# Joining the two transposes of a block and their ScalarE copies in a gated attention kernel

## The chip, the cores and the metric

The kernel runs on one core of one Trainium2 chip. The metric is the device time of one execution in microseconds, given as the median of several runs. The engines are named as the profile names them: PE is TensorE's matmul, PEld its weight load, DVE is VectorE, ACT is ScalarE, POOL is GpSimd, SP issues the DMAs.

## What is computed

The input `x` has 16 batches of 64 channels by 512 positions; the context has the same shape. Everything is fp32. Cut to what matters:

```python
# attention, per batch: q = layernorm(x), k = c = s = context
qp = Wq @ instance_norm(q) + bq            # 64 x 512
kp = Wk @ instance_norm(k) + bk
sp = Ws @ s + bs_
attn = softmax(qp^T @ kp, axis=-1)         # 512 x 512
mean, mean_sq = attn-weighted sums of sp and of sp*sp
x = x + tanh(g_xattn) * (instance_norm(c) * sqrt(relu(mean_sq - mean**2)) + mean)
# feed-forward with a dequantised 512 x 512 weight
x = x + tanh(g_ffn) * (layernorm(x) @ w.T)
```

## The kernel before

Two batches of 64 channels fill the 128 partitions, so there are 8 tiles `t` (`TILES`), each with batches `b` = 0 and 1. The 512 query positions of a tile are cut into 4 blocks `j` of 128 (`JC`), which gives 32 pairs `g = 4t + j` (`PAIRS`); a pair is one block of queries for both batches. Each engine runs its own hand-written instruction list strictly in order, and semaphores order the engines against each other.

For one pair: `scores(g)` on PE (line 250) writes 128x1024 scores, both batches side by side, into one of two two-bank PSUM tiles; `maximum(g)` on DVE (line 558) reduces both halves in one instruction; `exponentials(g, b)` on ACT (line 394) writes `probs` and its row sum, one batch at a time; `reciprocal(g, b)` on DVE and `normalise_probs(g, b)` on POOL divide by the sum; `turn(g, b)` on PE (line 265) transposes the four 128x128 blocks of one batch into the bank `turn_bank[b]`; `keep_turned(g, b)` on ACT (line 403) copies that bank into `probs_t`; and one tile later `weigh(t, b, i)` on PE (line 275) multiplies `probs_t` with the values. Four `weigh` calls make the sums of one batch of a tile, which `keep_sums` (line 411) copies out.

The lists interleave the pairs. In the loop step `g`:

- PE runs, where `j` is even, `scores(g+2)` and `scores(g+3)`; then `project_q` (`j` = 0), `project_k` (`j` = 1) or `value_product` (`j` = 2); then `turn(g, 0)` and `turn(g, 1)`, and two `weigh` calls of the tile before. Where `j` is odd, one `weigh` stands between the two turns and one behind them.
- ACT runs `keep_sums` (`j` = 0 and 2), `keep_q_hi` (`j` = 0, it waits for `project_q`) or `keep_k_hi` (`j` = 1); then `exponentials(g+2, 0)`, `keep_turned(g, 0)`, `exponentials(g+2, 1)`, `keep_turned(g, 1)`.
- DVE runs `reciprocal(g+1, 1)`, then `maximum(g+2)`, then the statistics and splits of later tiles.

So `maximum` of a pair stands behind the reciprocal of batch 1 of the pair before, and that reciprocal waits for `exponentials(.., 1)` of that pair. `scores(g)` waits until `exponentials(g-2, 1)` has read its score tile (`exp_done`, line 256). `turn(g, b)` waits until the copy of the same bank, one pair earlier, is done (line 269). After the loop come the last sums, the roots, the second layer norm and the feed-forward (`turn_y`, `feed_forward`), whose `y` and `result` tiles lie in `probs_t`.

In the first pairs the lists are written out by hand (lines 303 to 314 on PE): `scores(2)`, `turn(0, 0)`, `scores(3)`, `turn(0, 1)`, `project_k_plain(1)`, `turn(1, 0)`, `turn(1, 1)`; on ACT `keep_k_hi(1)` stands between `keep_turned(1, 0)` and `exponentials(3, 1)` (line 447), and `scores(4)` waits for `keep_k_lo(1)` on DVE, which waits for that `keep_k_hi(1)`.

Of the kernel before, what the change touches and what calls it, by code (L numbers as in the profile page):

```python
# [14 lines left out]
P = 128  # L15


def gated_attention_ffn(nc, x, context, params, weight_q_t, scales_zeros, out):


    BATCHES, C, N = x.shape
    TILES = BATCHES // 2
    JC = N // P
    PAIRS = JC * TILES
# [3 lines left out]
    PROBS = 6  # L28
# [8 lines left out]
    with ExitStack() as ctx:  # L37
        def sb(name, shape, dt=F32):
            return ctx.enter_context(nc.sbuf_tensor(name, shape, dt))

        def banks(name, n=1):
            return ctx.enter_context(nc.psum_tensor(name, [P, n * 512], F32))

        def sem(name):
            return ctx.enter_context(nc.semaphore(name))
# [29 lines left out]
        probs = [sb(f"probs{i}", [P, N]) for i in range(PROBS)]  # L75
        neg_max = sb("neg_max", [P, 4, 2])
        den = sb("den", [P, 4, 2])
        rden = sb("rden", [P, 4, 2])
        probs_t = [[sb(f"probs_t{i}{b}", [P, JC, N]) for b in range(2)] for i in range(2)]
        values = [sb(f"values{i}", [P, JC, 2, 2, C]) for i in range(2)]  # L80
        mean_sq = sb("mean_sq", [P, N])

        ident = sb("ident", [P, P])
# [12 lines left out]
        rstd2 = sb("rstd2", [P, TILES])  # L96
        shift2 = sb("shift2", [P, TILES])

        y = [probs_t[0][0][:, i, :] for i in range(4)]
        result = [probs_t[0][1][:, i, :] for i in range(4)]  # L100
        yt_hi = q_hi
        yt_lo = q_lo

        score = [banks(f"score{i}", 2) for i in range(2)]
        turn_bank = [banks(f"turn_bank{i}") for i in range(2)]
        pv_bank = banks("pv_bank")
        proj_bank = banks("proj_bank")
        ffn_bank = [score[i][:, n:n + 512] for n in (0, 512) for i in range(2)]
# [41 lines left out]
        probs_done = sem("probs_done")  # L150
        turned = sem("turned")
        turned_kept = sem("turned_kept")
        pv_done = sem("pv_done")
# [30 lines left out]
        def sums_bank(t, b):  # L184
            return proj_bank if (t, b) == (TILES - 1, 0) else pv_bank
# [34 lines left out]
        def _(pe):  # L220
# [41 lines left out]
                                         k[n][half(b), :], start=(n == 0), stop=(n == 2))  # L262
                last.then_inc(scores_done, 1)

            def turn(g, b):
                c = 2 * g + b
                pe.wait_ge(probs_done, c + 1)
                if c >= 2:
                    pe.wait_ge(turned_kept, c - 1)
                for i in range(JC):  # L270
                    last = pe.transpose(turn_bank[b][:, P * i:P * i + P],  # L271
                                        probs[c % PROBS][:, P * i:P * i + P], ident[:, :])
                last.then_inc(turned, 1)

            def weigh(t, b, i):
                if i == 0:
                    pe.wait_ge(turned_kept, 2 * (JC * t + JC - 1) + b + 1)
                    pe.wait_ge(s_squared, t + 1)
                    if sums_bank(t, b) is proj_bank:
                        pe.wait_ge(s_kept, t + 1)  # L280
                    elif (t, b) == (0, 0):
                        pe.wait_ge(k_lo_done, 1)
                    else:
                        pe.wait_ge(sums_kept, min(2 * (2 * t + b), 4 * (TILES - 1)))
                mm = pe.matmul(sums_bank(t, b)[:, :], values[t % 2][:, i, b, :, :].rearrange("p a c -> p (a c)"),  # L285
                               probs_t[t % 2][b][:, i, :], start=(i == 0), stop=(i == JC - 1))
                if i == JC - 1:
                    mm.then_inc(pv_done, 1)

# [16 lines left out]
            scores(1)  # L306
            project_q_plain(1)
            scores(2)
            turn(0, 0)
            scores(3)  # L310
            turn(0, 1)
            project_k_plain(1)
            turn(1, 0)
            turn(1, 1)
            pe.wait_ge(w_split, 1)

            for t in range(TILES):
                for j in range(JC):
                    g = JC * t + j
                    if g < 2:  # L320
                        continue
                    if j % 2 == 0 and g + 2 < PAIRS:
                        scores(g + 2)
                        scores(g + 3)
                    if j == 0 and t + 1 < TILES:
                        project_q(t + 1)
                    if j == 1 and t + 1 < TILES:
                        project_k(t + 1)
                    if j == 2:
                        value_product(t)  # L330
                    turn(g, 0)
                    if t > 0 and j % 2 == 1:
                        weigh(t - 1, j // 2, 2)
                    turn(g, 1)
                    if t > 0 and j % 2 == 1:
                        weigh(t - 1, j // 2, 3)
                    if t > 0 and j % 2 == 0:
                        weigh(t - 1, j // 2, 0)
                        weigh(t - 1, j // 2, 1)

            def turn_y(u):
                pe.wait_ge(y_done, u + 1)
                if u < 2:
                    pe.wait_ge(turned_kept, 2 * PAIRS)
                else:
                    pe.wait_ge(yt_lo_done, u - 1)
                for g in range(GROUPS):
                    last = pe.transpose(turn_bank[u % 2][:, P * g:P * g + P], y[u % 4][:, P * g:P * g + P],
                                        ident[:, :])
                last.then_inc(y_turned, 1)  # L350
# [30 lines left out]
        def _(act):  # L381
# [18 lines left out]
                               bias=neg_max[:, g % 4, b:b + 1],  # L400
                               accum_out=den[:, g % 4, b:b + 1]).then_inc(exp_done, 1)

            def keep_turned(g, b):
                t, j = g // JC, g % JC
                act.wait_ge(turned, 2 * g + b + 1)
                if j == 0 and t >= 2:
                    act.wait_ge(pv_done, 2 * (t - 2) + b + 1)
                act.copy(probs_t[t % 2][b][:, :, P * j:P * j + P],  # L408
                         turn_bank[b][:, :].rearrange("p (i n) -> p i n", i=JC)).then_inc(turned_kept, 1)

            def keep_sums(t, b):
                act.wait_ge(pv_done, 2 * t + b + 1)
# [6 lines left out]
            def root(u):  # L419
                act.wait_ge(relu_done, u + 1)  # L420
                act.activation(VAR[:, u, :], VAR[:, u, :], ACT.Sqrt).then_inc(root_done, 1)  # L421
# [11 lines left out]
            for t in range(TILES):  # L433
                for j in range(JC):
                    g = JC * t + j
                    if j == 0 and t >= 2:
                        keep_sums(t - 2, 1)
                    if j == 2 and t >= 1:
                        keep_sums(t - 1, 0)
                    if j == 0 and 0 < t < TILES - 1:  # L440
                        keep_q_hi(t + 1)
                    if j == 1 and 0 < t < TILES - 1:
                        keep_k_hi(t + 1)
                    if g + 2 < PAIRS:
                        exponentials(g + 2, 0)
                    keep_turned(g, 0)
                    if g == 1:
                        keep_k_hi(1)
                    if g + 2 < PAIRS:
                        exponentials(g + 2, 1)  # L450
                    keep_turned(g, 1)
                    if g == PAIRS - 2:
                        root(0)

# [472 lines left out]
```

## Time and profile before

| | us |
|---|---|
| median of 3 runs | 179.69 |
| lowest and highest of them | 179.33, 180.91 |
| the profiled execution | 180.87 |
| its span, first to last instruction | 178.7 |

The span is what the trace shows; 2.17 us of the profiled execution lie around it. Starts in the trace are counted in us from the start of the span. Instructions on one engine overlap a little, so the distance between two starts, not the duration of one row, tells what an instruction costs its queue. The end of a matmul is modelled. A wait is put down to what came last.

### The profile page before, as it was taken

How to read it: one execution, taken by the hardware profiler on the slowest of the kernel's cores; microseconds unless marked ns; L12 is line 12 of the kernel's file. 1: busy time of each engine (PE TensorE's matmuls, PEld its weight loads, DVE VectorE, ACT ScalarE, POOL GpSimd, SP SyncE). 2: the span in 40 equal slices, each digit the busy share in tenths (PEclk: the TensorE clock that was granted, in tenths of full speed). 3: DMA queues.
4: the chain of work that ended last, by engine and by line, in shares of the span. 5: the costliest groups of instructions: out<-in, count | busy, mean ns of one | idle time of the engine just before them, and what ended most of it. 6: DMA issues, size and time to landing. Idle time of an engine off the chain costs nothing.

```text
span 178.7 us, 2695 instructions
## 1 busy us (share of the span) xinstructions
PE 164.8 (92%) x832; PEld 108.1 (60%) x832; DVE 136.8 (77%) x277; ACT 123.3 (69%) x268; POOL 131.4 (74%) x155
## 2 busy tenths in 40 slices
PE   6768596999999999999999999999999999998992
PEld 6335473756667566656666575667656546866881
DVE  2899757776699779977987997777567579999941
ACT  2439737787788888778778887796889987723410
POOL 1407729656969997998899799996889899994100
PEclk9999969999999999999999999999999999999999
DMA  5991013005000400310000000000000000101323
GB/s 167 354 397 72 0 44 133 4 2 176 0 0 4 178 0 0 109 71 0 2 4 2 0 0 0 0 4 0 0 0 2 0 0 4 54 5 71 129 97 117
DMA packets 4717, 9.83 MB, mean 55 GB/s; under 512 B 480, under 2 KB 608, under 8 KB 4704
## 3 DMA queue, kind: packets, MB, share of 16 engines
q1 hardware_dynamic: 4704, 9.67, 14.9%
q8 instruction: 7, 0.11, 0.3%
q14 instruction: 6, 0.05, 0.1%
HBM read 7.57 MB, written 2.10 MB: 54 GB/s over the span
## 4 chain that ended last, share of the span: by engine, by line
PE 69%; DVE 14%; POOL 8%; ACT 5%; issue 2%; DMA 1%; ACTq 0%; POOLq 0%
PE pv_bank L285 25%; PE score L261 13%; PE turn_bank L271 13%; PE proj_bank L295 5%; ACT probs L399 3%; DVE X L687 2%; PE score L362 2%; POOL CTX L858 2%; DVE neg_max L560 2%; DVE stats L692 2%; PE score L358 2%; PE score L359 2%; DVE probs_t L711 2%; DMA X<-in_x 1%; POOL rstd L862 1%
## 5 line engine op out<-in xcount | busy, mean ns | idle before, releaser
L768 POOL TENSOR_SCALAR probs<-probs,rden 128x512 f32<-128x512 f32 x64 | 51.8, 815 | 12.1 <-DVE rden L565 12.1
L285 PE MATMUL pv_bank<-probs_t,values 128*128 128x512 f32 x120 | 58.8, 594 | 0.4 <-ACT VAR L417 0.4
L399 ACT ACTIVATE probs<-score,neg_max 128x512 f32<-128x512 f32 x64 | 44.3, 692 | 18.7 <-DVE neg_max L560 18.7
L560 DVE TENSOR_REDUCE neg_max<-score 128x2 f32<-128x1024 f32 x32 | 38.6, 1209 | 3.9 <-PE score L261 3.9
L271 PEld LDWEIGHTS turn_bank<-ident,probs 128*128 128x128 f32 x256 | 30.7, 142 | 16.1 <-issue 13.6
L408 ACT COPY probs_t<-turn_bank 128x512 f32<-128x512 f32 x64 | 37.4, 586 | 2.5 <-PE turn_bank L271 2.5
L271 PE MATMUL turn_bank<-ident,probs 128*128 128x128 f32 x256 | 36.3, 275 | 0.9 <-ACT probs_t L408 0.9
L285 PEld LDWEIGHTS pv_bank<-probs_t,values 128*128 128x128 f32 x120 | 19.4, 191 | 8.8 <-issue 8.8
L261 PE MATMUL score<-k_hi,q_hi 64*128 64x512 f32 x64 | 14.7, 450 | 5.8 <-DVE k_lo L554 3.6
L565 DVE RECIPROCAL rden<-den 128x1 f32<-128x1 f32 x64 | 9.6, 151 | 10.5 <-ACT probs L399 10.2
L261 PEld LDWEIGHTS score<-k_hi,q_hi 64*128 64x128 f32 x64 | 6.1, 183 | 18.0 <-issue 10.8
L358 PE MATMUL score<-w_hi,q_hi 128*128 128x512 f32 x32 | 13.2, 414 | 0.2 <-ACT q_hi L468 0.2
L261 PE MATMUL score<-k_hi,q_lo 64*128 64x512 f32 x64 | 13.1, 400 | 0.0
L261 PE MATMUL score<-k_lo,q_hi 64*128 64x512 f32 x64 | 13.0, 396 | 0.0
L399 ACT ACTIVATION_READ_ACCUMULATOR probs<-score,neg_max 128x1 f32 x64 | 12.9, 202 | 0.0
L359 PE MATMUL score<-w_lo,q_hi 128*128 128x512 f32 x32 | 12.7, 396 | 0.0
L461 ACT ACTIVATE probs_t<-X,shift,rstd 128x512 f32<-128x512 f32 x8 | 6.5, 817 | 7.4 <-POOL shift L865 7.3
L745 POOL TENSOR_TENSOR rstd<-var_eps,power 128x1 f32<-128x1 f32 x8 | 4.4, 550 | 9.3 <-DVE var_eps L507 9.3
L858 POOL TENSOR_TENSOR CTX<-CTX,VAR 128x512 f32<-128x512 f32 x8 | 10.7, 1332 | 0.7 <-ACT VAR L421 0.6
L749 POOL TENSOR_TENSOR rstd<-var_eps,power 128x1 f32<-128x1 f32 x8 | 6.3, 788 | 6.1 <-DVE var_eps L516 6.1
L787 POOL TENSOR_TENSOR VAR<-VAR,mean_sq 128x512 f32<-128x512 f32 x8 | 10.6, 1323 | 0.2
L548 DVE SCALAR_TENSOR_TENSOR q_lo<-proj_bank,params_sb,q_hi 128x512 fp32r<-128x512 f32 x8 | 6.0, 750 | 6.1 <-ACT q_hi L386 6.1
(85 smaller groups left out, 298.3 us busy)
## 6 DMA issues: line engine op xcount, KB each, us to landing
X<-in_x SPq DMA_DIRECT2D x8, 256.0 KB, 5.3
raw_ctx<-in_context SPq DMA_DIRECT2D x8, 256.0 KB, 2.7
sz<-in_scales_zeros SPq DMA_DIRECT2D x4, 512.0 KB, 3.7
out<-probs_t SPq DMA_DIRECT2D x8, 256.0 KB, 2.0
w_int<-in_weight_q_t SPq DMA_DIRECT2D x1, 1024.0 KB, 8.3
params_sb<-in_params SPq DMA_DIRECT2D x1, 226.0 KB, 3.9
```

Source lines behind the costliest of these rows:

```text
L261: last = pe.matmul(score[g % 2][:, N * b:N * b + N], q[n][half(b), P * j:P * j + P], k[n][half(b), :], start=(n == 0), stop=(n == 2))
L271: last = pe.transpose(turn_bank[b][:, P * i:P * i + P], probs[c % PROBS][:, P * i:P * i + P], ident[:, :])
L285: mm = pe.matmul(sums_bank(t, b)[:, :], values[t % 2][:, i, b, :, :].rearrange("p a c -> p (a c)"), probs_t[t % 2][b][:, i, :], start=(i = ...
L358: pe.matmul(ffn_bank[u % 4], hi, w_hi[:, g, :], start=(g == 0), stop=False)
L359: pe.matmul(ffn_bank[u % 4], hi, w_lo[:, g, :], start=False, stop=False)
L399: act.activation(probs[c % PROBS][:, :], score[g % 2][:, N * b:N * b + N], ACT.Exp, bias=neg_max[:, g % 4, b:b + 1], accum_out=den[:, g % ...
L408: act.copy(probs_t[t % 2][b][:, :, P * j:P * j + P], turn_bank[b][:, :].rearrange("p (i n) -> p i n", i=JC)).then_inc(turned_kept, 1)
L560: dve.tensor_reduce(neg_max[:, g % 4, :], score[g % 2][:, :].rearrange("p (b m) -> p b m", b=2), AX_X, ALU.max, negate=True).then_inc(max_ ...
L565: dve.reciprocal(rden[:, g % 4, b:b + 1], den[:, g % 4, b:b + 1]).then_inc(rden_done, 1)
L768: pool.tensor_scalar(probs[c % PROBS][:, :], probs[c % PROBS][:, :], rden[:, g % 4, b:b + 1], 1.0, ALU.mult, ALU.mult).then_inc(probs_done, 1)
L787: pool.tensor_tensor(VAR[:, t, :], VAR[:, t, :], mean_sq[:, :], ALU.subtract).then_inc(var_done, 1)
L858: pool.tensor_tensor(CTX[:, u, :], CTX[:, u, :], VAR[:, u, :], ALU.mult).then_inc(scaled_done, 1)
```

## The change

The two turns of a pair become one function that waits once for `turned_kept` and then runs the eight transposes in a row, batch 0 into the first and batch 1 into the second of two neighbouring banks (`turn_banks`). `keep_turned(g)` is one ACT copy of both banks, 128x1024, in place of two of 128x512, and it waits until both batches are turned. The `probs_t` tiles of both batches become one tile. The copy stands where the first of the two copies stood, between the two exponentials. `turned_kept` now counts pairs. On PE, where `j` is odd, both `weigh` calls follow the turns; in the first pairs `turn(0, 1)` moves ahead of `scores(3)`.

```diff
-        probs_t = [[sb(f"probs_t{i}{b}", [P, JC, N]) for b in range(2)] for i in range(2)]
+        probs_t = [sb(f"probs_t{i}", [P, 2, JC, N]) for i in range(2)]
...
-        turn_bank = [banks(f"turn_bank{i}") for i in range(2)]
+        turn_banks = banks("turn_banks", 2)
+        turn_bank = [turn_banks[:, 512 * i:512 * i + 512] for i in range(2)]
...
-            def turn(g, b):
-                c = 2 * g + b
-                pe.wait_ge(probs_done, c + 1)
-                if c >= 2:
-                    pe.wait_ge(turned_kept, c - 1)
-                for i in range(JC):
-                    last = pe.transpose(turn_bank[b][:, P * i:P * i + P],
-                                        probs[c % PROBS][:, P * i:P * i + P], ident[:, :])
-                last.then_inc(turned, 1)
+            def turn(g):
+                if g >= 1:
+                    pe.wait_ge(turned_kept, g)
+                for b in range(2):
+                    c = 2 * g + b
+                    pe.wait_ge(probs_done, c + 1)
+                    for i in range(JC):
+                        last = pe.transpose(turn_bank[b][:, P * i:P * i + P],
+                                            probs[c % PROBS][:, P * i:P * i + P], ident[:, :])
+                    last.then_inc(turned, 1)
...
-                    pe.wait_ge(turned_kept, 2 * (JC * t + JC - 1) + b + 1)
+                    pe.wait_ge(turned_kept, JC * t + JC)
...
             scores(2)
-            turn(0, 0)
+            turn(0)
             scores(3)
-            turn(0, 1)
             project_k_plain(1)
-            turn(1, 0)
-            turn(1, 1)
+            turn(1)
...
-                    turn(g, 0)
-                    if t > 0 and j % 2 == 1:
-                        weigh(t - 1, j // 2, 2)
-                    turn(g, 1)
-                    if t > 0 and j % 2 == 1:
-                        weigh(t - 1, j // 2, 3)
-                    if t > 0 and j % 2 == 0:
-                        weigh(t - 1, j // 2, 0)
-                        weigh(t - 1, j // 2, 1)
+                    turn(g)
+                    if t > 0:
+                        weigh(t - 1, j // 2, 2 * (j % 2))
+                        weigh(t - 1, j // 2, 2 * (j % 2) + 1)
...
-            def keep_turned(g, b):
+            def keep_turned(g):
                 t, j = g // JC, g % JC
-                act.wait_ge(turned, 2 * g + b + 1)
+                act.wait_ge(turned, 2 * g + 2)
                 if j == 0 and t >= 2:
-                    act.wait_ge(pv_done, 2 * (t - 2) + b + 1)
-                act.copy(probs_t[t % 2][b][:, :, P * j:P * j + P],
-                         turn_bank[b][:, :].rearrange("p (i n) -> p i n", i=JC)).then_inc(turned_kept, 1)
+                    act.wait_ge(pv_done, 2 * (t - 2) + 2)
+                act.copy(probs_t[t % 2][:, :, :, P * j:P * j + P],
+                         turn_banks[:, :].rearrange("p (b i n) -> p b i n", b=2, i=JC)).then_inc(turned_kept, 1)
...
                     if g + 2 < PAIRS:
                         exponentials(g + 2, 0)
-                    keep_turned(g, 0)
+                    keep_turned(g)
                     if g == 1:
                         keep_k_hi(1)
                     if g + 2 < PAIRS:
                         exponentials(g + 2, 1)
-                    keep_turned(g, 1)
```

## Rows read from the trace of the kernel before

**Rows 1.** The page: busy us of each engine, then TensorE's granted clock in 40 slices.
```profile
PE 164.8 (92%) x832; PEld 108.1 (60%) x832; DVE 136.8 (77%) x277; ACT 123.3 (69%) x268; POOL 131.4 (74%) x155
...
PEclk9999969999999999999999999999999999999999
```

**Rows 2.** Waits of PE, 40 to 140 us: waiter <- waited for: us, times, longest.
```profile
PE pv_bank L285 <- ACT VAR L417: 0.4, 1, 0.4
```

**Rows 3.** Waits of ACT, 40 to 140 us.
```profile
ACT probs L399 <- DVE neg_max L560: 12.1, 18, 0.9
```

**Rows 4.** Timeline, 80 to 98 us: start us, us, engine, line, operation [idle before <-releaser].
```profile
80.99 0.69 ACT L386 ACTIVATE q_hi<-proj_bank,params_sb 128x512 fp32r<-128x512 f32 x1 [0.99 <-PE proj_bank L239]
...
82.24 0.58 ACT L408 COPY probs_t<-turn_bank 128x512 f32<-128x512 f32 x1
...
83.97 1.20 DVE L560 TENSOR_REDUCE neg_max<-score 128x2 f32<-128x1024 f32 x1
...
86.35 0.70 ACT L399 ACTIVATE probs<-score,neg_max 128x512 f32<-128x512 f32 x1
...
87.33 0.20 PEld L261 LDWEIGHTS score<-k_hi,q_hi 64*128 64x128 f32 x2
...
89.36 1.04 PE L271 MATMUL turn_bank<-ident,probs 128*128 128x128 f32 x8
...
90.69 0.70 ACT L399 ACTIVATE probs<-score,neg_max 128x512 f32<-128x512 f32 x1
...
91.52 0.14 PEld L271 LDWEIGHTS turn_bank<-ident,probs 128*128 128x128 f32 x1 [0.24 <-issue]
91.59 1.21 DVE L560 TENSOR_REDUCE neg_max<-score 128x2 f32<-128x1024 f32 x1
...
92.83 0.69 ACT L399 ACTIVATE probs<-score,neg_max 128x512 f32<-128x512 f32 x1 [0.88 <-DVE neg_max L560]
...
93.51 0.57 ACT L408 COPY probs_t<-turn_bank 128x512 f32<-128x512 f32 x1
...
93.97 0.70 ACT L399 ACTIVATE probs<-score,neg_max 128x512 f32<-128x512 f32 x1
...
95.20 0.19 PEld L261 LDWEIGHTS score<-k_hi,q_hi 64*128 64x128 f32 x2
...
96.22 0.19 PEld L237 LDWEIGHTS proj_bank<-x_hi,w_qk_hi 128*128 128x128 f32 x1 [0.36 <-issue]
...
97.21 0.69 ACT L386 ACTIVATE q_hi<-proj_bank,params_sb 128x512 fp32r<-128x512 f32 x1 [0.76 <-PE proj_bank L239]
```

**Rows 5.** Timeline, 12 to 34 us: the first pairs, before the steady stretch.
```profile
18.04 1.04 PE L271 MATMUL turn_bank<-ident,probs 128*128 128x128 f32 x8
...
19.27 0.70 ACT L391 ACTIVATE k_hi<-proj_bank,params_sb 128x512 fp32r<-128x512 f32 x1
...
21.01 0.50 PE L261 MATMUL score<-k_hi,q_hi 64*128 64x512 f32 x2 [1.93 <-DVE k_lo L554]
...
24.89 1.31 PE L271 MATMUL turn_bank<-ident,probs 128*128 128x128 f32 x8
...
26.28 0.69 ACT L399 ACTIVATE probs<-score,neg_max 128x512 f32<-128x512 f32 x1
...
29.56 0.70 ACT L399 ACTIVATE probs<-score,neg_max 128x512 f32<-128x512 f32 x1
...
30.40 0.19 PEld L261 LDWEIGHTS score<-k_hi,q_hi 64*128 64x128 f32 x2 [1.62 <-ACT probs L399]
...
31.30 0.19 PEld L237 LDWEIGHTS proj_bank<-x_hi,w_qk_hi 128*128 128x128 f32 x1 [0.37 <-issue]
```

**Rows 6.** Timeline of ACT, 0 to 12 us: a shorter cast and an activation.
```profile
5.57 0.41 ACT L424 CAST w_qk_hi<-params_sb 128x256 fp32r<-128x256 f32 x1 [3.57 <-DMA params_sb<-in_params]
5.88 0.20 ACT L425 ACTIVATE tanh_g<-params_sb 128x2 f32<-128x2 f32 x1
```

**Rows 7.** Timeline, 124 to 134 us: an exponential near the end of the loop.
```profile
130.49 0.70 ACT L399 ACTIVATE probs<-score,neg_max 128x512 f32<-128x512 f32 x1
```

More of the change, by code:

```diff
@@ L97, in gated_attention_ffn @@
         shift2 = sb("shift2", [P, TILES])
-        y = [probs_t[0][0][:, i, :] for i in range(4)]
-        result = [probs_t[0][1][:, i, :] for i in range(4)]
+        y = [probs_t[0][:, 0, i, :] for i in range(4)]
+        result = [probs_t[0][:, 1, i, :] for i in range(4)]
         yt_hi = q_hi
@@ L285, in weigh @@
                 mm = pe.matmul(sums_bank(t, b)[:, :], values[t % 2][:, i, b, :, :].rearrange("p a c -> p (a c)"),
-                               probs_t[t % 2][b][:, i, :], start=(i == 0), stop=(i == JC - 1))
+                               probs_t[t % 2][:, b, i, :], start=(i == 0), stop=(i == JC - 1))
                 if i == JC - 1:
@@ L343, in turn_y @@
                 if u < 2:
-                    pe.wait_ge(turned_kept, 2 * PAIRS)
+                    pe.wait_ge(turned_kept, PAIRS)
                 else:
```

## The prediction

> **What bounds the kernel now.** I read the page's busy times first. PE is busy 164.8 us of 178.7, ACT only 123.3 [rows 1]: work taken from ACT as such buys nothing. The waits of PE from 40 to 140 us show one wait of 0.4 us [rows 2], so in that stretch PE's own work sets the time. The waits of ACT there are mostly for `neg_max`, 18 times, 12.1 us together [rows 3]: ACT is short of input, not of time. So the question is not how much ACT is spared, but whether its results still reach PE in time. For that I took the timeline of one tile, t = 4 [rows 4].
>
> A tile lasts from one `keep_q_hi` (80.99) to the next (97.21), 16.22 us. Beside PE's work a chain of latencies runs through it, once around per pair: exponential 0, copy of batch 0, exponential 1, reciprocal, maximum of the next pair, exponential 0 of that pair. Its steps, start to start, from [rows 4]: exponential 0 to copy 0.68 (92.83 to 93.51); copy to exponential 1 0.46 (93.51 to 93.97); exponential 1 to next maximum 0.90 (90.69 to 91.59); maximum to exponential 0 1.24 (91.59 to 92.83). The second copy is not in it: it lies in the shadow of the maximum. And twice a tile PE's second `scores` of a step needs exponential 1 of the pair two earlier. How long after the exponential's start that release comes, the first pairs show: 29.56 to 30.40, 0.84, and there it is PE that waits [rows 5]. In the tile, the exponentials at 86.35 and 93.97 release at 87.19 and 94.81, and the loads they gate start at 87.33 and 95.20. The chain has slack of 0.14 and 0.39 us. That is what the change has to fit in.
>
> **What the change does to the terms.**
>
> The joint copy. No 128x1024 ACT copy is in the trace. That one instruction may read two neighbouring banks, the 128x1024 maximum shows (1.20 us, one row, 83.97) [rows 4]. Its price is the step of 0.46 plus 512 more elements. From the 128x256 cast, 0.41 us, to the 128x512 copy, 0.58, an element costs 0.66 ns, so 512 of them +0.34. From the 128x2 activation, 0.20, to the 128x512 exponential, 0.69, it is 0.96 ns, +0.49 [rows 4, 6]; but more than a second copy in the queue, +0.47, I don't expect. I take +0.43, a step of 0.89, in the upper half, since the exponential has the copy's length and the cast has not. Ends: 0.80 and 0.93.
>
> Per pair, ACT's queue spends 0.89 where it spent 2 x 0.46: nearly nothing is saved. But the chain has 0.89 where it had 0.46, since the half that lay in the maximum's shadow now stands ahead of exponential 1.
>
> The wait for both turns. The copy needs the eighth transpose. With j = 2 these start at 89.36 and end 1.04 later, 90.40 [rows 4]; so far the copy needed the fourth only, and then ACT, not PE, was last. For the other steps I take the turns as ended before exponential 0 is, since what ACT waits for is the maximum [rows 3]. PE's moved `weigh` calls cost nothing: eight transposes and four weighs, the same in any order. `turn(g)` now waits for the joint copy of the pair before; in j = 3 that is its tightest place, worked out below. Where j is odd, `probs` of batch 1 is wanted earlier by the length of one `weigh`; I take it as ready, since PE never waits for POOL in 100 us [rows 2].
>
> Walk through a tile, with the new step. The copy of pair j = 0 starts at 82.24 as before; exponential 1 at 83.13; maximum 0.90 on, 84.03 (so far 83.97); exponential 0 1.24 on, 85.27; copy 85.95; exponential 1 86.84; release 0.84 on, 87.68. The load so far started at 87.33. A gated load wins back 0.12: from it to the next stage's load it is 0.90 (30.40 to 31.30) [rows 5], ungated 1.02 (95.20 to 96.22) [rows 4]. So PE is late by 87.68 - 87.33 - 0.12 = 0.23. Everything PE does then moves by that, the turns of j = 2 too: they end at 90.63. Copy 90.65, exponential 1 91.54 (so far 90.69), maximum 92.44, exponential 0 93.68, copy 94.36, exponential 1 95.25, release 96.09. PE is late by 96.09 - 95.20 - 0.12 = **0.77**, and `keep_q_hi`, which waits for PE, comes at 97.98. The next tile starts late by just that and runs the same path, so each tile adds 0.77. The turns of j = 3, whose first load is at 91.52, now 91.75, want the joint copy that runs from 90.65 to about 91.66: hidden, by 0.1; where that cover fails PE waits for tenths, which the upper end of the range takes in. Behind the late exponentials come their reciprocals and POOL's `normalise_probs`, which PE wants only in the next step but one.
>
> The first pairs [rows 5]. The turns of pair 1 start at 18.04 and end at 19.08. So far `keep_k_hi(1)` stood behind the first copy, at 19.27; now copy at 19.10, `keep_k_hi(1)` at 19.99: +0.72, and PE is idle there, waiting for `k_lo` (1.93 us ahead of 21.01). Then the turns of pair 2 end at 24.89 + 1.31 + 0.72 = 26.92; copy 26.94; exponential 1 27.83 (so far 26.28); maximum 28.73; exponential 0 29.97; copy 30.65; exponential 1 31.54; release 32.38 in place of 30.40. The start loses **1.98**.
>
> The steady tiles: from `keep_q_hi` of t = 1 to that of t = 6 there are five rounds: 5 x 0.77 = **3.85**.
>
> The end. From `keep_q_hi` of t = 6 (97.21 + 16.22 = 113.43) exponential 1 of j = 3 comes 14.26 later (95.25 - 80.99), 127.69; maximum 128.59, exponential 0 129.83, copy 130.51, exponential 1 of pair 30 131.40; the row has it at 130.49 [rows 7]. Behind it the last maximum, exponential and POOL's list follow to the end of attention, and the tail keeps that **0.91**.
>
> Sum: 1.98 + 3.85 + 0.91 = 6.74. Against the profiled span of 178.7 that is 185.4, and with the 2.17 us around it 187.6; that execution (180.87) was 1.18 above the median, so against the median 179.69 + 6.7 = **186.4**.
>
> The bounds: a tile has four copies in the path, the start three, the end five. With a step of 0.80 a tile loses 0.77 - 4 x 0.09 = 0.41 and all is 2.05 + 1.71 + 0.46 = 4.2 (183.9); with 0.93 it is 0.93 a tile, 4.65 + 2.10 + 1.11 = 7.9 (187.6).
>
> What the Trainium skill says of such edits speaks on both sides (Perfetto Trace Analysis, Optimizing Scalar/DVE Operations): larger operations spare a fixed cost per instruction and help if the engine is saturated; an engine that is not saturated but causes bubbles elsewhere is better served by breaking instructions up. By the first the time would fall, which is the rival "faster" below; by the second it would rise. The waits of ACT side with the second.
>
> **The rivals.**
>
> Faster: ACT is the bound after all. The joint copy is some 1.01 us (0.58 + 0.43) against 2 x 0.58, 0.15 less, 32 times: 4.8 us of ACT's time, and 174.9 if all came through. Against it: ACT idles 12.1 us for the maximum [rows 3], PE waits 0.4 in 100 us [rows 2], and in queue time the saving is 0.03 a pair, 1 us. It decides only where ACT has no idle ahead of the exponential. The Trainium skill's section just named stands behind this rival.
>
> Hidden in the tiles: the joint copy's step is 0.70 or less, that is 0.47 ns for an added element. Then a tile's 0.77 falls to zero (4 x 0.19), the end to about zero, and the start to 1.98 - 3 x 0.19 = 1.4: 181.1. For it: the slack is a matter of tenths. Against it: both slopes of [rows 6] are above 0.47.
>
> The clock falls once more. PE's granted clock is 6 tenths in one slice of 4.5 us, just behind PE's idle stretch of the first pairs [rows 1, 5]. The change makes that stretch longer and puts gaps of 0.77 in each tile. One more such slice costs 0.4 x 4.5 = 1.8: 188.1. Against it: the idle of the weight load ahead of 30.40, 1.62 us, stands in a slice of 9 tenths with another behind it.
>
> **How the numbers follow.** Forecast 0.74, clock 0.09, hidden 0.09, faster 0.04, something that costs more than all of these 0.04. The range 183.0 to 189.0 holds forecast and clock, 0.83; it takes in both ends of the copy's price (183.9, 187.6) with 0.9 and 1.4 us beyond for the walk and the thin cover at j = 3. A measurement of this kernel can tell about 1% from no change. Hidden is within 1%: same 0.09, faster 0.04, slower 0.87.
>
> **What would show it.** In the profile after: the 128x1024 copy at about 1.01 us, its step to the next exponential 0.89; PE's `scores` waiting for `probs` of ACT twice a tile (0.2 to 0.3, and 0.6 or more), where it waits for nothing now; a tile of 16.99 us from `keep_q_hi` to `keep_q_hi`; `keep_k_hi(1)` near 20.0; ACT still waiting for `neg_max`. Wrong would be: a tile of 16.2 us, no waits of `scores`, or a copy step under 0.75.

## The result, and the profile after

| us | before | after |
|---|---|---|
| median | 179.73 (4 runs) | 189.97 (4 runs) |
| lowest, highest | 179.33, 180.91 | 189.21, 191.61 |
| the profiled execution | 180.87 | 189.28 |
| its span | 178.7 | 187.1 |

The changed kernel takes 1.057 times as long (95% interval 1.049 to 1.065). The forecast said slower, by the chain of latencies; that is what happened. The time is 3.6 us above the forecast and 1.0 us above the top of its range.

The page of the changed kernel, busy times, granted clock and the row of the new copy:

```profile
PE 168.3 (90%) x832; PEld 108.0 (58%) x832; DVE 134.9 (72%) x277; ACT 122.5 (65%) x236; POOL 130.2 (70%) x155
...
PEclk9999998899999999999999999999999999999999
...
L403 ACT COPY probs_t<-turn_banks 128x1024 f32<-128x1024 f32 x32 | 32.2, 1007 | 4.1 <-PE turn_banks L273 4.1
```

ACT has 32 instructions fewer and 0.8 us less work than in [rows 1], and the kernel is 10 us slower. The joint copy lasts 1.007 us, as the forecast's 1.01 had it.

Waits of the changed kernel from 40 to 140 us, of PE, of its weight load and of ACT (waiter <- waited for: us, times, longest); [rows 2, 3] are the same view of before:

```profile
PE score L262 <- ACT probs L394: 1.7, 6, 0.3
...
PEld score L262 <- ACT probs L394: 11.2, 18, 0.8
...
PEld turn_banks L273 <- ACT probs_t L403: 1.7, 7, 0.2
...
ACT probs L394 <- DVE neg_max L554: 14.9, 18, 1.4
...
ACT probs_t L403 <- PE turn_banks L273: 3.2, 6, 0.8
```

In the kernel before, the weight load's line reads:

```profile
PEld score L261 <- ACT probs L399: 3.0, 4, 0.8
```

So the loads of `scores` now find the exponential late 18 times instead of 4, that is three times a tile (0.40, 0.76 and 0.72 in each steady tile). The 0.76 is the wait that four tiles of the kernel before have too; PE itself, which was still at work on the stage before, idled behind none of the four. [rows 2] show PE alone, and so the forecast's "it waits for nothing now" missed these waits of the load. ACT waits longer for the maximum, and longer for the turns: 3.2 us where it was 0.7. ACT, DVE and POOL have less work than before; PE's 832 matmuls are the same and last 3.5 us longer. What has changed is that everybody is later.

One tile of the changed kernel, t = 4, in the timeline (start us, us, engine, line, operation, [idle before <-releaser]); it answers to [rows 4], with all times 4.60 later:

```profile
85.59 0.69 ACT L381 ACTIVATE q_hi<-proj_bank,params_sb 128x512 fp32r<-128x512 f32 x1 [0.73 <-PE proj_bank L240]
...
86.84 1.01 ACT L403 COPY probs_t<-turn_banks 128x1024 f32<-128x1024 f32 x1
87.73 0.71 ACT L394 ACTIVATE probs<-score,neg_max 128x512 f32<-128x512 f32 x1
...
91.45 0.70 ACT L394 ACTIVATE probs<-score,neg_max 128x512 f32<-128x512 f32 x1
...
92.30 0.19 PEld L262 LDWEIGHTS score<-k_hi,q_hi 64*128 64x128 f32 x2 [0.40 <-ACT probs L394]
...
95.27 1.01 ACT L403 COPY probs_t<-turn_banks 128x1024 f32<-128x1024 f32 x1 [0.27 <-PE turn_banks L273]
96.17 0.69 ACT L394 ACTIVATE probs<-score,neg_max 128x512 f32<-128x512 f32 x1
...
97.07 1.21 DVE L554 TENSOR_REDUCE neg_max<-score 128x2 f32<-128x1024 f32 x1
...
98.31 0.69 ACT L394 ACTIVATE probs<-score,neg_max 128x512 f32<-128x512 f32 x1 [1.35 <-DVE neg_max L554]
...
99.88 0.70 ACT L394 ACTIVATE probs<-score,neg_max 128x512 f32<-128x512 f32 x1
...
100.72 0.19 PEld L262 LDWEIGHTS score<-k_hi,q_hi 64*128 64x128 f32 x2 [0.72 <-ACT probs L394]
...
102.61 0.69 ACT L381 ACTIVATE q_hi<-proj_bank,params_sb 128x512 fp32r<-128x512 f32 x1 [0.73 <-PE proj_bank L240]
```

From copy to exponential 1 is 0.89 (86.84 to 87.73) where it was 0.46. Read downwards, this is the chain: exponential 1 at 91.45 releases the load at 92.30; the turns that follow PE's late `scores` hold the copy back to 95.27; exponential 1 at 96.17, maximum at 97.07, exponential 0 at 98.31, exponential 1 at 99.88, release at 100.72. The tile lasts 17.02 (85.59 to 102.61).

The first pairs, ACT and PE; it answers to [rows 5]:

```profile
19.53 1.01 ACT L403 COPY probs_t<-turn_banks 128x1024 f32<-128x1024 f32 x1 [0.21 <-PE turn_banks L273]
20.44 0.69 ACT L386 ACTIVATE k_hi<-proj_bank,params_sb 128x512 fp32r<-128x512 f32 x1
...
22.17 0.50 PE L262 MATMUL score<-k_hi,q_hi 64*128 64x512 f32 x2 [2.68 <-DVE k_lo L548]
...
24.75 1.04 PE L273 MATMUL turn_banks<-ident,probs 128*128 128x128 f32 x8
...
30.43 0.70 ACT L394 ACTIVATE probs<-score,neg_max 128x512 f32<-128x512 f32 x1
...
31.27 0.79 PE L262 MATMUL score<-k_hi,q_hi 64*128 64x512 f32 x2 [2.39 <-ACT probs L394]
...
34.30 0.90 PE L273 MATMUL turn_banks<-ident,probs 128*128 128x128 f32 x6
34.54 0.69 ACT L381 ACTIVATE q_hi<-proj_bank,params_sb 128x512 fp32r<-128x512 f32 x1 [3.31 <-PE proj_bank L240]
```

And the turns of pair 4 in the kernel before:

```profile
32.11 1.03 PE L271 MATMUL turn_bank<-ident,probs 128*128 128x128 f32 x8
```

`keep_q_hi(1)` comes at 34.54, before at 32.31: 2.23 lost. The two idle stretches of PE, 2.68 and 2.39, are longer than before. Behind the second one the records of `scores` are long, 0.79 instead of 0.50: the clock is at its lower level, 1.2 GHz.

Sum over the spans: start 2.23; from `keep_q_hi(1)` to the last `keep_k_hi` (116.73, now 122.92, 6.19 later in all) 3.96; from there to the end 61.97 before and 64.18 now, 2.21. Together 8.4.

The end loses more than the tiles explain. POOL and DVE at the start of the second layer norm, changed kernel:

```profile
146.52 2.62 POOL L852 TENSOR_TENSOR CTX<-CTX,VAR 128x512 f32<-128x512 f32 x2
...
147.82 1.86 DVE L681 SCALAR_TENSOR_TENSOR X<-CTX,tanh_g,X 128x512 f32<-128x512 f32 x1 [3.39 <-POOL CTX L852]
```

and the kernel before:

```profile
140.56 0.75 DVE L687 SCALAR_TENSOR_TENSOR X<-CTX,tanh_g,X 128x512 f32<-128x512 f32 x1 [2.39 <-POOL CTX L858]
...
141.18 1.27 POOL L858 TENSOR_TENSOR CTX<-CTX,VAR 128x512 f32<-128x512 f32 x1 [0.65 <-ACT VAR L421]
```

Before, POOL idled 0.65 between `scale_context(0)` and `scale_context(1)`, waiting for ACT's root, and DVE's first `X` started in that gap. In the changed kernel that root comes 6.7 us later than before and POOL's first `scale_context` 7.3 us later, so the root is no longer the last: POOL runs both in a row, and DVE's instruction beside the second lasts 1.86 instead of 0.75, 1.11 more.

### The profile page after: what moved, and what is told of

It reads as the page before. It is cut to its first block, busy times and chain, and to the rows that moved or that the text cites. A ratio compares the mean times of both kernels' runs of the same rounds, so it can differ in the third digit from the quotient of the medians.

```text
span 187.1 us, 2626 instructions
## 1 busy us (share of the span) xinstructions
PE 168.3 (90%) x832; PEld 108.0 (58%) x832; DVE 134.9 (72%) x277; ACT 122.5 (65%) x236; POOL 130.2 (70%) x155
## 4 chain that ended last, share of the span: by engine, by line
PE 51%; DVE 19%; ACT 11%; issue 9%; POOL 8%; ACTq 0%; POOLq 0%
PE score L262 11%; PE pv_bank L287 11%; PE turn_banks L273 9%; ACT probs L394 8%; DVE neg_max L554 7%; PE proj_bank L297 4%; DVE X L681 3%; PE turn_banks L303 2%; ACT probs_t L403 2%; PE score L357 2%; POOL CTX L852 2%; PE proj_bank L238 2%; DVE stats L686 2%; PE score L354 2%; PE score L353 2%
## 5 line engine op out<-in xcount | busy, mean ns | idle before, releaser
L762 POOL TENSOR_SCALAR probs<-probs,rden 128x512 f32<-128x512 f32 x64 | 50.1, 785 | 20.3 <-DVE rden L559 20.1
L287 PE MATMUL pv_bank<-probs_t,values 128*128 128x512 f32 x120 | 56.5, 593 | 0.6 <-ACT VAR L412 0.6
L403 ACT COPY probs_t<-turn_banks 128x1024 f32<-128x1024 f32 x32 | 32.2, 1007 | 4.1 <-PE turn_banks L273 4.1
L273 PEld LDWEIGHTS turn_banks<-ident,probs 128*128 128x128 f32 x256 | 29.6, 141 | 8.7 <-issue 3.8
L273 PE MATMUL turn_banks<-ident,probs 128*128 128x128 f32 x256 | 33.4, 274 | 1.1 <-ACT probs_t L403 1.1
L287 PEld LDWEIGHTS pv_bank<-probs_t,values 128*128 128x128 f32 x120 | 20.5, 190 | 15.6 <-issue 15.6
L262 PE MATMUL score<-k_hi,q_hi 64*128 64x512 f32 x64 | 16.1, 498 | 9.4 <-ACT probs L394 5.1
L681 DVE SCALAR_TENSOR_TENSOR X<-CTX,tanh_g,X 128x512 f32<-128x512 f32 x8 | 8.8, 1094 | 4.1 <-POOL CTX L852 4.1
L381 ACT ACTIVATE q_hi<-proj_bank,params_sb 128x512 fp32r<-128x512 f32 x8 | 5.5, 689 | 9.1 <-PE proj_bank L240 7.0
L739 POOL TENSOR_TENSOR rstd<-var_eps,power 128x1 f32<-128x1 f32 x8 | 4.4, 549 | 9.5 <-DVE var_eps L501 9.5
```

The costliest lines, as they stand in the source:

```text
L262: last = pe.matmul(score[g % 2][:, N * b:N * b + N], q[n][half(b), P * j:P * j + P], k[n][half(b), :], start=(n == 0), stop=(n == 2))
L273: last = pe.transpose(turn_bank[b][:, P * i:P * i + P], probs[c % PROBS][:, P * i:P * i + P], ident[:, :])
L403: act.copy(probs_t[t % 2][:, :, :, P * j:P * j + P], turn_banks[:, :].rearrange("p (b i n) -> p b i n", b=2, i=JC)).then_inc(turned_kept, 1)
L681: dve.scalar_tensor_tensor(X[:, u, :], CTX[:, u, :], tanh_g[:, 0:1], X[:, u, :], ALU.mult, ALU.add).then_inc(x2_done, 1)
L762: pool.tensor_scalar(probs[c % PROBS][:, :], probs[c % PROBS][:, :], rden[:, g % 4, b:b + 1], 1.0, ALU.mult, ALU.mult).then_inc(probs_done, 1)
```

## The experiments

The theory: the second half of the copy has moved from the maximum's shadow into the chain exponential 0, copy, exponential 1, maximum. Against it stood the number of instructions, the order on PE, the joined wait, and the clock.

**Place or length.** The joined turns stay; two 128x512 copies stand at the old places, each waiting for both turns.

```diff
-                    keep_turned(g)
+                    keep_turned(g, 0)
...
                         exponentials(g + 2, 1)
+                    keep_turned(g, 1)
```

> The changed kernel with its turns joined as they are, but the copy taken apart again: batch 0 behind exponential 0, batch 1 behind exponential 1, both waiting for both turns. Theory (the second half of the copy stands in the chain exponential 0, copy, exponential 1, maximum): the tile falls from 17.02 us back to 16.2, PE's scores no longer wait in the steady stretch, and only the start keeps 0.5 to 1 us from the wait for both turns: 180.2 to 181.0, a ratio to before of 1.003 to 1.008. Rival (the joined turns, their wait and the moved weigh calls are the cost): still 188 or more, a tile near 17 us.

The median of its four executions is 185.77, but two of them had a granted clock of 0.843 (the profiled one, 197.99) and 0.934. The other two took 183.30 and 184.43, a ratio of 1.022 (1.015 to 1.029): above the 180.2 to 181.0 of the theory and under the 188 of the rival, so neither was right. A profile at a higher clock had to show why:

> The kernel of the first experiment once more, for a profile at full granted clock, since the first profile of it had a clock of 0.84. It has joined turns and split copies, and its best run was 183.3 where 180.2 to 181.0 was expected. New theory: the joined turn of j = 3 waits for both copies of the pair before, and the second of them now stands behind exponential 1; PE reaches these turns 0.4 to 0.6 us too early, so a tile is 16.7 to 16.9 us with PE waiting for probs_t of ACT. Rival (the loss is all in the first pairs): a tile of 16.2 us and keep_k_hi of tile 1 late by 3 us.

184.24 (one execution, granted clock 0.991), and a tile of 16.57 (`keep_q_hi` from 33.25 to 116.10 in five), a little under the 16.7 to 16.9 expected. ACT, then the weight load, in this kernel's timeline:

```profile
93.58 0.59 ACT L403 COPY probs_t<-turn_banks 128x512 f32<-128x512 f32 x1
...
94.22 0.86 PEld L273 LDWEIGHTS turn_banks<-ident,probs 128*128 128x128 f32 x8 [0.94 <-ACT probs_t L403]
```

and the load's waits from 40 to 130 us:

```profile
PEld turn_banks L273 <- ACT probs_t L403: 6.8, 11, 0.9
```

What the first forecast for this kernel missed: a joined `turn(g)` waits for both copies of the pair before, and with the second copy behind a late exponential 1 the turn of j = 3 is 0.94 late. With the copies at these places the joined turn has a price of its own, 0.35 a tile (16.57 against 16.22). Against the profiled execution of the kernel before that is 1.7 of 3.3 us; the start has 0.9 of the rest and the end 0.6. Two copies between the exponentials remove that and keep the place:

> The changed kernel with two copies of 128x512 in place of the one of 128x1024, both between the exponentials. Theory (what counts is what stands between the exponentials, not how many instructions it is): two steps of 0.46 or 0.47 against one of 0.89, 0.04 more for each copy of the chain, 0.16 a tile: a tile of 17.2 us and 1 us slower than the changed kernel, about 191. Rival (one long read over two banks is slow or holds PE up by itself): clearly faster than the changed kernel, 185 or less.

190.88, 0.9 above the changed kernel. Its ratio, 1.057, is the same within the intervals, but its tile is 17.26 against 17.02. Its ACT timeline:

```profile
88.91 1.07 ACT L403 COPY probs_t<-turn_banks 128x512 f32<-128x512 f32 x2
89.85 0.72 ACT L394 ACTIVATE probs<-score,neg_max 128x512 f32<-128x512 f32 x1
```

Two small copies in that place cost 0.94 of chain, the joint one 0.89. So making one copy of two spares 0.05 a pair and harms nothing by itself, and taking it apart without moving the second half gains nothing; the place does the harm. The opposite test puts the joint copy behind exponential 1:

```diff
-                    keep_turned(g)
...
                         exponentials(g + 2, 1)
+                    keep_turned(g)
```

> The changed kernel with the joint copy moved behind exponential 1, where the maximum of the next pair (1.2 us) covers it. Theory: the chain is now shorter than that of the kernel before (no copy in it), PE bounds the tile again at 16.2 us, and the first pairs gain since exponential 1 and k_hi no longer stand behind a copy: 177.5 to 179.5. Rival (the joint copy or the wait for both turns hurts wherever it stands, since the next turn waits for it): 183 or more with PE waiting for the copy.

178.72 over 10 runs (ratio 0.9934, 0.9913 to 0.9955), with the granted clock at 0.997 or more in each. ACT's timeline:

```profile
87.38 0.69 ACT L394 ACTIVATE probs<-score,neg_max 128x512 f32<-128x512 f32 x1 [0.91 <-DVE neg_max L554]
...
88.06 0.68 ACT L394 ACTIVATE probs<-score,neg_max 128x512 f32<-128x512 f32 x1
...
88.72 1.01 ACT L403 COPY probs_t<-turn_banks 128x1024 f32<-128x1024 f32 x1
...
90.60 0.69 ACT L394 ACTIVATE probs<-score,neg_max 128x512 f32<-128x512 f32 x1 [0.86 <-DVE neg_max L554]
```

The exponentials stand 0.68 apart, and the same copy of 1.01 lies wholly in the wait for the maximum: the tiles last 16.22 to 16.29. The whole loss is gone with one line moved.

Length alone, at the change's place: from pair 8 on only the first bank is copied, so batch 1 of tiles 2 to 7 is weighed with old values.

```diff
+                if g < 8:
+                    act.copy(probs_t[t % 2][:, :, :, P * j:P * j + P],
+                             turn_banks[:, :].rearrange("p (b i n) -> p b i n", b=2, i=JC)).then_inc(turned_kept, 1)
+                else:
+                    act.copy(probs_t[t % 2][:, 0, :, P * j:P * j + P],
+                             turn_bank[0].rearrange("p (i n) -> p i n", i=JC)).then_inc(turned_kept, 1)
```

> The changed kernel, but from pair 8 on (tiles 2 to 7) the ACT copy takes only the first of the two banks, so batch 1 is weighed with stale values in these tiles; the wait for both turns and its place between the exponentials stay. Theory (the added 512 elements between the exponentials are what costs): the tile of tiles 2 to 6 is 16.2 to 16.3 us in place of 17.0, and the time 4.0 us under the changed kernel, 185.5 to 186.5. Rival (the wait for both turns costs part of it): a tile of 16.5 or more.

The median is 185.76, inside the expectation; `keep_q_hi` comes at 52.84, 69.06, 85.28, 101.50, 117.72: 16.22 a tile, the value of before, with joined turns and joined waits in place. The length of what stands there is the whole loss of the tiles.

**The order on PE alone:** eight transposes in a row and the `weigh` calls behind, with separate waits and copies as before.

> Only PE's order is changed against the kernel before: the eight transposes of a pair stand in a row and the weigh calls behind them, but each batch has its own copy and its own waits, as before. Theory (the order by itself costs nothing in the steady stretch): a tile of 16.2 to 16.4 us and 179.5 to 181.5. Rival (what the first experiment lost comes from the order of PE and not from the waits for both batches): 183 or more.

180.31 over 10 runs, ratio 1.0022 (0.9983 to 1.0061), tile 16.22: the order is free, as forecast. Five of the ten had a granted clock of 0.99 and took 180.73 to 181.12; the other five had 0.998 or more and took 179.32 to 179.90.

**The end.** POOL's second `scale_context` waits for DVE's first `X`:

```diff
             scale_context(0)
+            pool.wait_ge(x2_done, 1)
             scale_context(1)
```

> The changed kernel with one wait more: POOL's scale_context(1) waits until DVE's after_attention(0) is done. In the trace of the changed kernel that DVE instruction (X<-CTX, line 681) took 1.86 us against 0.75 before, with POOL's scale_context(1) running at the same time; before, POOL stood idle there for a root of ACT. Theory (the two get in each other's way at a shared memory port): the instruction is back at 0.75 and the end gains about 1.1 us, 188.9. Rival (it is slow for another reason, or the wait gives the gain back): 189.7 to 190.5 and the instruction still at 1.8.

DVE, then POOL, in this kernel's timeline:

```profile
150.18 0.75 DVE L681 SCALAR_TENSOR_TENSOR X<-CTX,tanh_g,X 128x512 f32<-128x512 f32 x1 [3.39 <-POOL CTX L852]
...
151.01 1.28 POOL L852 TENSOR_TENSOR CTX<-CTX,VAR 128x512 f32<-128x512 f32 x1 [0.86 <-DVE X L681]
```

0.75 again, and from the last `keep_k_hi` to the end 62.75 instead of 64.18. The median, 189.67, does not show it: it was expected at 188.9, and it lies in the range of the rival. The granted clocks of this kernel are 0.973 to 0.988; in its profiled execution the first pairs ran at a low clock, and `keep_q_hi(1)` came at 35.55, 1.0 later. The page's clock of this kernel:

```profile
PEclk9999788599999999999999999999999999999999
```

**The clock.** Matmuls of the identity, whose result nobody reads, fill PE's two idle stretches of the first pairs, 18 in each, behind `turn(1)` and ahead of `scores(7)`:

```diff
+            for _ in range(18):
+                pe.matmul(pv_bank[:, 0:P], ident[:, :], ident[:, :], start=True, stop=True)
```

> The changed kernel with 18 small matmuls into an unused bank at each of the two places of the first pairs where PE is idle longest (behind turn(1), and ahead of scores(7)); their results are not used. Theory (part of the loss is TensorE's granted clock, which falls behind these idle stretches: runs of the changed kernel show 0.97 to 0.99, those of the kernel before 0.99 to 1.00): the clock is 0.998 or more in all runs, the time 186.8 to 188.0, that is 2 to 3 us under the 189.97 of the changed kernel, and the tile is still 17.0 us. Rival (the clock's dip is no cost of its own): 189.5 to 190.5.

189.66, no gain, though the clock stayed up (0.997 to 1.0). The number is the rival's, the reason is not. PE's timeline says why:

```profile
19.14 4.18 PE L316 MATMUL pv_bank<-ident 128*128 128x128 f32 x36
23.26 0.50 PE L262 MATMUL score<-k_hi,q_hi 64*128 64x512 f32 x2
...
29.89 4.29 PE L328 MATMUL pv_bank<-ident 128*128 128x128 f32 x36
34.11 0.51 PE L262 MATMUL score<-k_hi,q_hi 64*128 64x512 f32 x2
```

Each fp32 matmul of this size makes two records of 0.116: 18 last 4.2 us, in gaps of 2.4 to 2.7. `scores(7)` starts at 34.11, while exponential 1 of pair 5, at 31.53, had released it by 32.37 (0.84 later).

This profile also bears on the end. POOL's wait is not in this kernel, and yet DVE's first `X` lasts 0.75:

```profile
149.29 0.75 DVE L686 SCALAR_TENSOR_TENSOR X<-CTX,tanh_g,X 128x512 f32<-128x512 f32 x1 [2.40 <-POOL CTX L857]
...
149.41 1.78 POOL L857 TENSOR_TENSOR CTX<-CTX,VAR 128x512 f32<-128x512 f32 x1 [0.15 <-ACT VAR L421]
```

Here ACT's root was the last by 0.15, DVE started 0.12 ahead of POOL, and POOL bore the delay (1.78 for 1.27); the end takes 63.06. In e2_two_between it is the same (0.75, and 1.66 on POOL; 63.3). So the 1.11 are not a fixed price of the change: tenths decide which of the two comes first.

With 10 in each:

> As the run with 18 small matmuls at two idle places of the first pairs, with 10 at each. There the 36 weight loads and matmuls took 4.18 and 4.29 us, 0.116 us each, and overran the gaps: scores(4) came 1.2 us and scores(7) 1.7 us after what they wait for. Ten take 2.3 us and fit. Theory: clock 1.0 in all runs as there, without the 3 us of overrun: 186.5 to 187.3, which is 2.7 to 3.5 under the changed kernel's 189.97. Rival (the dip of the clock costs nothing on the path): 189 or more.

187.67 (187.58 to 188.24), 0.4 above the expectation's upper end, 2.3 below the changed kernel. The granted clock is 0.998 to 1.0 in its runs, 0.97 to 0.99 in those of the changed kernel. That the gain is the clock's, and not that of the added matmuls as such, e2_two_between shows without any: its one execution at 1.0 took 188.35, its three at 0.979 to 0.982 took 190.84 to 190.99. The page's clock with 10 in each gap:

```profile
PEclk9999999999999999999999999999999999999999
```

And both together, 10 matmuls in each gap and POOL's wait:

> The changed kernel with the ten small matmuls at both places and with POOL's scale_context(1) waiting for DVE's after_attention(0). These are the two things that the forecast left out, so what stays should be the forecast's own sum: the undisturbed kernel before, 179.6, plus 1.98 + 3.85 + 0.91 = 186.3, a range of 185.9 to 186.8, and a tail from keep_k_hi of tile 6 to the end of 62.9 us. Rival (the sum was wrong in its own terms too): 187.2 or more.

186.31 (186.02 to 186.51; ratio 1.033), with a tile of 17.01 and 62.7 from the last `keep_k_hi` to the end. With the clock and the collision taken out, the sum of the forecast stands: 6.7 above the 179.6 that before takes where its clock stays up. Its terms stand too. Against the profiled execution of e9_order_only, which has the tiles of before and whose clock stayed up, `keep_q_hi(1)` comes 2.07 later (32.83 and 30.76), the five tiles take 3.98 more (85.08 and 81.10) and the end 0.7 more (62.7 and 62.05); the forecast had 1.98, 3.85 and 0.91.

**Part of the start.** On that kernel, with 4 matmuls in the first gap, `keep_k_hi(1)` goes ahead of the joint copy:

> As the run before in this list, with keep_k_hi(1) of ACT ahead of keep_turned(1) in the first pairs (and 4 small matmuls in place of 10 in the gap, which gets shorter). Theory (scores(4) waits for k_hi(1), which stands behind the joint copy): k_hi(1) 1.2 us earlier, and all behind it: 1.0 to 1.3 us faster than that run, about 185.1. Rival (the chain through exponential 1 of the first pairs sets the start): no gain, within 0.3.

184.65, a gain of 1.66 where 1.0 to 1.3 was expected. `keep_k_hi(1)` comes at 18.72 instead of 20.07, 1.35 earlier, and PE's wait for `k_lo` shrinks to 0.55. The two profiled executions differ by 1.5: `keep_q_hi(1)` comes 1.38 earlier, of which 0.13 lies ahead of the first exponential, and the end is 0.10 shorter. So the start gained 1.25, as expected; the last 0.2 of the medians is in neither profile.

**The better version.** The kernel before, nothing joined, both copies behind exponential 1:

```diff
-                    keep_turned(g, 0)
                     if g == 1:
                         keep_k_hi(1)
                     if g + 2 < PAIRS:
                         exponentials(g + 2, 1)
+                    keep_turned(g, 0)
                     keep_turned(g, 1)
```

> The kernel before with nothing joined, but both of its copies behind exponential 1. Theory (what makes the third experiment 1.1 us faster than the kernel before is the place of the copy in the first pairs, not that it is one instruction): 178.3 to 179.3, as the third experiment. Rival (the joint copy brings the gain, since two copies take 0.04 us more of the queue and PE waits for the second): 179.5 or more.

178.11 (178.05 to 178.27), ratio 0.989 (0.984 to 0.995): the lowest median of all. Its timeline at the start, ACT and PE:

```profile
18.91 0.68 ACT L391 ACTIVATE k_hi<-proj_bank,params_sb 128x512 fp32r<-128x512 f32 x1
...
20.64 0.50 PE L261 MATMUL score<-k_hi,q_hi 64*128 64x512 f32 x2 [1.45 <-DVE k_lo L554]
...
27.82 0.50 PE L261 MATMUL score<-k_hi,q_hi 64*128 64x512 f32 x2 [0.84 <-ACT probs L399]
```

`scores(7)` starts at 27.82 instead of 30.40 [rows 5]. Its tiles are 16.22 like before's, so the steady tiles gain nothing: there the chain had slack already. Nearly all of the gain is in the first pairs, where PE waits for the chain: shorter waits, and a clock that does not fall (0.998 to 1.0 in all its runs). Of the 2.8 between the profiled executions 2.6 lie ahead of `keep_q_hi(1)`, 1.3 of them in the low clock of before, and 0.2 at the end. The median is 0.6 under that of the same place with a joint copy (178.72), but the two ran on different chips, and the intervals of their ratios overlap. Between their profiled executions (0.9 apart) 0.37 lies ahead of the first exponential, where PE's first projection took 1.45 and 1.10, 0.13 in the tiles and 0.42 at the end. So joining at the good place has not been shown to gain anything, nor to lose more than tenths.

## Why the forecast was right, and where it fell short

**What bounds the kernel: right.** PE with a chain of latencies beside it, ACT short of input. Less work for ACT was worth nothing; the rival "faster" (174.9) had the instruction count right and the place wrong. The Trainium skill (Perfetto Trace Analysis, Optimizing Scalar/DVE Operations) gives both halves: grouping for a saturated engine, breaking up for one that causes bubbles on others. This trace sides with the second, by 10 us, but only half of it: taken apart at the same place (e2_two_between) the copy cost no less, with a tile of 17.26 against 17.02, and joined behind exponential 1 (e3_copy_last) it cost nothing.

**The joint copy's step: right.** 0.89 was taken from between two slopes far apart (0.66 and 0.96 ns an element; the ends were 0.80 and 0.93), and 0.89 was measured. That it lay in the upper half was argued; that it fits to the hundredth is luck. The rival "hidden" needed 0.70.

**The tile: right.** The walk put the releases at 87.68 and 96.09; the trace has them at 92.30 and 100.72, less the shift of 4.60 that is 87.70 and 96.12. A tile of 16.99 was forecast, 17.02 measured. The thin cover at j = 3, 0.1, appears as seven waits of the turn's load for the copy, 1.7 us, at most 0.2 each, behind none of which PE's own row shows idle time. Of the sign "`scores` waiting twice a tile, 0.2 to 0.3, and 0.6 or more" PE's row shows one wait of 0.3 a tile; the load's row shows 0.40 and 0.72 at the two places. In e1_split_copies, where the copy moved back by the exponential's length, the same cover failed: 0.35 a tile. The prediction had named this place, the expectation for that run had not.

**The start: the sum near, by an exchange.** 1.98 forecast, 2.23 measured. `keep_k_hi(1)` comes 1.17 later, of which 0.40 belongs to a later first exponential (12.00 and 12.40). The input is not the reason: the cast that waits for its parameters started 0.54 earlier (5.03 and 5.57); PE's two matmuls of the first projection took 1.69 together where they took 1.10, at a place that the change does not touch. That leaves 0.77 against 0.72 forecast, and of the 2.23 of the start 1.83. But behind it the walk left the low clock where before has it: there `scores(4)` to the turns of pair 2 take 3.88 (21.01 to 24.89 [rows 5]). In the changed kernel they take 2.58 (22.17 to 24.75), the release forecast for 32.38 comes at 31.27, and the low clock lies behind it: from that load to the next turns 3.03 (31.27 to 34.30) instead of 1.71 (30.40 to 32.11). So 1.30 saved at one place was paid as 1.32 at the other. That the low clock lay in the first pairs of both profiled executions, and cost the same, is luck; the term itself is borne out where neither has it, 2.07 (e12_warm_and_wait against e9_order_only).

**The end: the first step that failed.** "The tail keeps that 0.91." The exponential of pair 30 comes at 137.68 instead of 130.49, 1.00 beyond the shift of 6.19; up to there the step held. But the tail lost 2.21. It was taken as a rigid list, moved as a whole. In fact the gap of 0.65 on POOL, which let DVE's first `X` run alone, was made by ACT's root, and the change moved POOL and ACT against each other, by 0.6 us in the profiled execution. With POOL's wait the tail is 62.7 to 62.75, against 62.88 forecast. This term is 1.3 of the error, and it is shown by the profile of e4_pool_waits and by the times of the pair e11_warm_ten and e12_warm_and_wait (187.67 and 186.31). That it fell so in each execution of the changed kernel is not shown, since one alone was traced and the end of e10_warm escaped it. The Trainium skill (Perfetto Trace Analysis, same section) says that GpSimd and DVE share an SBUF read port; the measured 1.86 against 0.75 fits that, though no run here separates the port from other causes.

**Base and clock: the second step that failed.** "That execution was 1.18 above the median, so against the median ..." The offset was carried over as if it were noise of one execution that both kernels share. It was the clock: of 33 executions of the kernel before that ran beside the experiments, 25 had a granted clock of 0.997 or more and a median of 179.62, and 8 had 0.99 and took 180.82 to 181.25; the profiled one (180.87) belongs to these, with its one slice of 6 tenths [rows 1]. The changed kernel had 0.97 to 0.99 in each of its four runs: what was the exception before became the rule. So the 1.18 should not have been taken off, and 0.7 more lies between the changed kernel's profiled execution (189.28) and its median. That is the rival "the clock falls once more" in part: it was given 0.09 and priced 1.8, and filling the gaps gave back 2.3. The forecast had the cause in sight, a longer idle stretch ahead of the fall, and dismissed it by one stretch that had not been followed by a fall.

**The sum.** 1.3 for the end, 0.4 for start and tiles together (as much as the changed kernel's first exponential came later), 1.2 for the offset and 0.7 for the lower clock make the 3.6 between 186.4 and 189.97. The experiments give the same without the profiles: 2.3 for the filled gaps and 1.4 for POOL's wait lead from 189.97 to 186.31. The range left them out because it was built from the copy's price and two reserves, 0.9 and 1.4 us, for the walk, with none for the end or the base.

## What to carry to other kernels

Before you join two instructions of an engine that has idle time, ask which of them lies in the shadow of a wait, and put the joined one there; a joined wait also takes the later of two inputs and frees the earlier of two buffers late. Move such work behind the instruction that others wait for, and try the move without the join first: here the move was the whole gain. Before you subtract the profiled execution's offset to the median, look whether its clock explains it, and do not move a tail as one piece when two engines in it are moved by different amounts.

## What the runs showed of the hardware

- One ACT copy from two neighbouring PSUM banks, 128x1024 fp32, lasts 1.007 us and takes 0.89 of the queue ahead of an exponential; two of 128x512 take 0.94.
- DVE's `scalar_tensor_tensor` of 128x512 fp32 lasts 0.75 us alone and 1.86 beside a POOL `tensor_tensor` of the same size that had started before it; POOL's two took 2.62 together, hardly more than 2 x 1.27. Where DVE had started 0.12 ahead (e10_warm) it took 0.75 and POOL 1.78. In both the one that came later bore the delay.
- The granted clock of the same kernel differs from run to run: 0.99 or about 1.0 before, 0.97 to 0.99 after. Leaving out the profiled execution of e1_split_copies (0.843) and the last slice of e2_two_between, it fell in the first pairs alone, behind idle stretches of PE of 1.9 to 2.7 us, and not behind each of them: in the changed kernel it stayed up behind 2.68 and fell behind 2.39. It did not fall in the steady tiles, where PE's gaps are up to 0.3. With ten small matmuls in each gap it stayed up in all four executions. One kernel without them, e2_two_between, took 188.35 us at 1.0 and some 2.5 us more at 0.98.
- An fp32 128x128 matmul on 128 columns costs PE 0.23 us, in two records.
